# Expert rows added by token into a DRAM sum as they leave PSUM, router weights held stationary

## What is computed

```python
x = _layernorm(x + attention(x))
logits = x @ W_router.T                      # 2048 x 8
probs = softmax(logits)
rw, sel = top_k(probs, 2)
combine = zeros((T, 8)).at[arange(T)[:, None], sel].add(rw)
sh = silu_and_mul(x @ Ws_gate_up) @ Ws_down  # inner width 1408
shared_out = sh * sigmoid(x @ W_sgate.T)
h = silu_and_mul(einsum('th,ehi->eti', x, We_gate_up))   # inner width 352, eight experts
eo = einsum('eti,eih->eth', h, We_down)
x = _layernorm(x + shared_out + einsum('eth,te->th', eo, combine))
```

## Time and profile before

| | us |
|---|---|
| median of 3 runs (lowest, highest) | 1134.67 (1134.11, 1134.91) |
| profiled execution: its own time | 1130.08 |
| profiled execution: span, first to last instruction | 1128.2 |
| PE busy in the span | 1054.4 (93%) |
| DVE busy | 767.7 (68%) |
| ACT busy | 632.9 (56%) |
| POOL busy | 412.1 (37%) |

### The profile page before, as it was taken

How to read it: one execution, slowest core, us unless ns; L and a number is a source line. 1 busy time by engine, 2 the same in 40 slices (tenths; PEclk the granted TensorE clock), 3 DMA queues, 4 the chain that set the end, 5 groups by cost and what they waited for, 6 DMA issues and landing times.

```text
span 1128.2 us, 19960 instructions
## 1 busy us (share of the span) xinstructions
PE 1054.4 (93%) x7180; PEld 874.4 (78%) x7180; DVE 767.7 (68%) x1173; ACT 632.9 (56%) x1287; POOL 412.1 (37%) x546
## 2 busy tenths in 40 slices
PE   4899999999999859998999999999999999999964
PEld 3677777777777648887888888888888888888853
DVE  4888787787777742593767676776867677773434
ACT  4566666666666633233565666666666666653333
POOL 4577887787777620001000010010001001004783
PEclk8899999999999996899899999999999999999988
DMA  5111111111111014135777898887888888856993
GB/s 198 42 39 31 31 31 37 53 31 31 31 31 49 20 30 139 38 122 186 225 255 241 258 280 291 256 266 260 261 263 262 289 270 260 266 170 162 234 185 110
DMA packets 125760, 175.80 MB, mean 156 GB/s; under 512 B 10624, under 2 KB 64256, under 8 KB 125664
## 3 DMA queue, kind: packets, MB, share of 16 engines
q1 hardware_dynamic: 117936, 155.92, 44.2%
q0 software_dynamic: 7728, 18.62, 7.0%
HBM read 155.90 MB, written 18.61 MB: 155 GB/s over the span
## 4 chain that ended last, share of the span: by engine, by line
PE 57%; DVE 2%; issue 1%; DMA 1%; ACT 0%; SPq 0%; POOL 0%; POOLq 0%; DVEq 0%; ACTq 0%
PE gate_ps L1299 4%; PE gate_ps L1300 3%; PE gate_ps L1301 3%; PE up_ps L1300 3%; PE up_ps L1301 3%; PE up_ps L1299 3%; PE down_ps L1326 3%; PE down_ps L1325 3%; PE down_ps L1324 3%; PE e_up_ps L1350 3%; PE e_up_ps L1351 2%; PE e_up_ps L1352 2%; PE e_gate_ps L1359 2%; PE e_up_ps L1359 2%; PE e_up_ps L1361 2%; PE e_gate_ps L1361 2%
## 5 line engine op out<-in xcount | busy, mean ns | idle before, releaser
L886 POOL DMA_INDIRECT rows<-x_dram,token_i x39 | 40.4, 1036 | 519.8 <-PE e_gate_ps L1341 424.0
L1182 DVE TENSOR_TENSOR e_lo<-e_raw,e_hi 128x1408 fp32r<-128x1408 f32 x78 | 126.5, 1623 | 45.8 <-ACT e_hi L955 45.8
L955 ACT CAST e_hi<-e_raw 128x1408 fp32r<-128x1408 f32 x78 | 107.5, 1379 | 55.8 <-PE e_up_ps L1361 55.8
L316 ACT ACTIVATE prob<-score_ps,nbias 128x256 f32<-128x256 f32 x256 | 119.8, 478 | 8.7 <-DVE nbias L412 8.6
L256 POOL TENSOR_TENSOR probT<-probT,masks 128x256 f32<-128x256 f32 x128 | 97.4, 782 | 67.1 <-DVE probT L433 67.0
L1187 DVE TENSOR_TENSOR ed_lo<-ed_raw,ed_hi 128x1024 fp32r<-128x1024 f32 x39 | 47.8, 1225 | 70.4 <-ACT ed_hi L963 70.4
L412 DVE TENSOR_REDUCE nbias<-score_ps 128x2 f32<-128x512 f32 x128 | 88.4, 691 | 4.4
L1299 PE MATMUL gate_ps<-x_hi,gu_lo 128*128 128x512 f32 x176 | 73.7, 419 | 18.0 <-issue 11.8
L324 ACT COPY probT<-probT_ps 128x512 f32<-128x512 f32 x64 | 37.6, 587 | 92.9 <-PE probT_ps L540 92.9
L506 PE MATMUL proj_ps<-wqkv_lo,xT_hi 128*128 128x512 f32 x180 | 79.4, 441 | 0.0
L904 POOL DMA_INDIRECT x1T<-expert_rows,slot_i x32 | 52.5, 1639 | 55.8 <-DMA expert_rows<-rows 45.2
(11 more groups left out here) (221 smaller groups left out, 2982.9 us busy)
## 6 DMA issues: line engine op xcount, KB each, us to landing
e_raw<-in_We_gu SPq DMA_DIRECT2D x78, 704.0 KB, 4.6
ed_raw<-in_We_down SPq DMA_DIRECT2D x39, 512.0 KB, 4.1
raw_ring<-in_Ws_gu SPq DMA_DIRECT2D x58, 256.0 KB, 5.5
wd_raw<-in_Ws_down SPq DMA_DIRECT2D x44, 256.0 KB, 5.0
expert_rows<-rows SPq DMA_DIRECT2D x39, 256.0 KB, 2.1
gu_raw<-in_Ws_gu SPq DMA_DIRECT2D x30, 256.0 KB, 5.0
ed_raw<-in_We_down SPq DMA_DIRECT2D x39, 192.0 KB, 4.7
xT_in<-in_xT SPq DMA_DIRECT2D x16, 256.0 KB, 2.8
```

What stands on the lines that cost most here:

```text
L316: nc.scalar.activation(prob[:, g % 2, h, :], score_ps[:, h, 0:2 * P], ACT.Exp, bias=nbias[:, s % 2, head:head + 1], scale=1.0, accum_out=r ...
L955: nc.scalar.copy(e_hi[:, half * HK:(half + 1) * HK, :], raw_half(i, half)).then_inc(e_hi_made, 1)
L1182: nc.vector.tensor_tensor(e_lo[:, part, :], raw_half(i, half), e_hi[:, part, :].bitcast(FP32), ALU.subtract).then_inc(e_lo_made, 1)
```

## The change

**Adding by token.** The result rows of a tile are no longer stored by slot and gathered at the end. A new DRAM tensor `sum_dram` holds one row a token, and 128 more for unused slots. `begin_sums` copies x into it at down 2, and `add_rows(i)` on POOL adds each tile's rows to it by an indirect DMA that scatters, right after the row is made. Each add waits for the one before. The token numbers for it (`target_i`) are `token_i`, with unused slots sent to the extra rows. At the end `load_sums` loads the sums of a quarter (1 MB) into `e_raw` by one plain DMA, at down 36 to 39, and POOL adds them to the shared part (`take_sums`) for the first three quarters, DVE for the last (`add_last`). The shared part leaves `down_ps` by ACT instead of DVE. The norm's numbers are made for a whole quarter, with `STATS_AT` = 38.

**Router.** `router_parts` holds a 128x32 block of router weights (`r_wide`, nine columns and zeros) stationary and moves 512 tokens. The four k-blocks of a quarter go to four groups of 32 PSUM partitions, so that the sum over k is left open; `take_parts` copies the banks to SBUF, and `join_logits` makes the sum and the transpose in one step, with 16 matmuls of nine columns (`join`). The parts run ahead of gate 0, the join after it.

**Earlier index.** `PREFIX_AT` goes from 3 to 2 and `INDEX_AT` from 7 to 6; `FIRST_TILE_AT` stays 9.

```diff
-    PREFIX_AT, INDEX_AT, FIRST_TILE_AT, STATS_AT = 3, 7, 9, 37
-
-    slots_dram = nc.dram_tensor("expert_rows", (TILES * P, H), FP32, kind="Internal").ap()
+    PREFIX_AT, INDEX_AT, FIRST_TILE_AT, SUMS_AT, STATS_AT = 2, 6, 9, 36, 38
+
+    sum_dram = nc.dram_tensor("sum_dram", (S + P, H), FP32, kind="Internal").ap()
...
+            def begin_sums():
+                sp.dma_start(sum_dram[0:S, :], x1_dram).then_inc(sum_begun, 16)
+                sp.dma_start(sum_dram[S:S + P, :], x1_dram[0:P, :]).then_inc(sum_begun, 16)
+
+            def load_sums(tt):
+                sp.wait_ge(rows_added, 16 * TILES)
+                if tt >= 2:
+                    sp.wait_ge(sum_taken, BT * (tt - 1))
+                at = tt % 2 * BT
+                sp.dma_start(sums[:, at:at + BT, :], sum_dram[tt * TN:(tt + 1) * TN, :].rearrange("(b p) n -> p b n", p=P)).then_inc(sum_loaded[tt], 16)
...
-            def store_rows(i):
-                sp.wait_ge(row_made, i + 1)
-                sp.dma_start(slots_dram[i * P:(i + 1) * P, :], rows[:, 2 + i % 2, :]).then_inc(rows_stored[i % 2], 16)
...
+            sp.wait_ge(r_cleared, 1)
+            sp.dma_start(r_wide[:, :, 0:NR], W_router_gate.rearrange("(k p) n -> p k n", p=P)).then_inc(router_loaded, 16)
+            sp.dma_start(tables[:, :], ident_in).then_inc(tables_loaded, 16)
             load_raw(1)
...
-                if stage == "down" and n % UN == 3:
-                    load_y(n // UN)
+                if stage == "down" and n == 2:
+                    begin_sums()
...
+                if stage == "down" and SUMS_AT <= n < SUMS_AT + NT:
+                    load_sums(n - SUMS_AT)
+                if stage == "down" and STATS_AT + 2 <= n < STATS_AT + 2 + NT - 1:
+                    for b in range(BT * (n - STATS_AT - 2), BT * (n - STATS_AT - 1)):
                         store_out(b)
...
+            def add_rows(i):
+
+                pool.wait_ge(row_made, i + 1)
+                if i:
+                    pool.wait_ge(rows_added, 16 * i)
+                pool.indirect_dma_start(sum_dram, bass.IndirectOffsetOnAxis(ap=target_i[:, i:i + 1], axis=0), rows[:, 2 + i % 2, :], None,
+                                        compute_op=ALU.add).then_inc(rows_added, 16)
+
             for i in range(TILES):
                 if i >= 2:
                     pool.wait_ge(xeT_mm, i - 1)
                 pool.indirect_dma_start(rows[:, i % 2, :], None, x1_dram, bass.IndirectOffsetOnAxis(ap=token_i[:, i:i + 1], axis=0)).then_inc(xe_loaded[i % 2], 16)
...
+                if i >= 2:
+                    add_rows(i - 2)
+            for i in range(TILES - 2, TILES):
+                add_rows(i)
+
+            def take_sums(tt):
+
+                pool.wait_ge(sum_loaded[tt], 16)
+                pool.wait_ge(evacuated, BT * (tt + 1))
+                for b in range(BT * tt, BT * (tt + 1)):
+                    nc.gpsimd.tensor_tensor(y_block(b), y_block(b), sums[:, b % (2 * BT), :], ALU.add).then_inc(sum_taken, 1)
...
+            for tt in range(NT - 1):
+                take_sums(tt)
+            for tt in range(NT - 1):
+                rstd_of(quarter(tt))
+                for b in quarter(tt):
+                    shift_of(b)
+            for b in quarter(NT - 1):
+                rstd_of([b])
+                shift_of(b)
...
             def copy_row(i):
                 act.wait_ge(ed_mm, i + 1)
                 if i >= 2:
-                    act.wait_ge(rows_stored[i % 2], 16 * (i // 2))
+                    act.wait_ge(rows_added, 16 * (i - 1))
...
+            def evacuate(b):
+
+                act.wait_ge(down_mm, BT * (UN * (b // BT) + UN - 1) + b % BT + 1)
+                act.wait_ge(x_lo_made, KT * (b // BT + 1))
+                act.wait_ge(part_mm, NT)
+                nc.scalar.activation(y_block(b), down_ps[b % BT][:, :], ACT.Identity, scale=shared[:, b:b + 1]).then_inc(evacuated, 1)
...
+            def router_parts():
+
                 pe.wait_ge(router_loaded, 16)
+                for tt in range(NT):
+                    for k in range(KT):
+                        lanes = slice(k * (P // KT), (k + 1) * (P // KT))
+                        last = nc.tensor.matmul(down_ps[tt][lanes, :], r_wide[:, k, :], x1T[:, k, tt * TN:(tt + 1) * TN], start=True, stop=True)
+                    last.then_inc(part_mm, 1)
+
+            def join_logits():
+
+                pe.wait_ge(part_taken, NT)
+                pe.wait_ge(tables_loaded, 16)
                 for b in range(NB):
-                    for k in range(KT):
-                        last = nc.tensor.matmul(e_up_ps[:, b * NR:(b + 1) * NR], x1T[:, k, b * P:(b + 1) * P], r_raw[:, k, :], start=(k == 0), stop=(k == KT - 1))
+                    last = nc.tensor.matmul(e_up_ps[:, b * NR:(b + 1) * NR], logit_parts[:, b * P:(b + 1) * P], join, start=True, stop=True)
                 last.then_inc(logit_mm, 1)
```

More of the change, by code:

```diff
@@ new lines, in rstd_of, with shift_of @@
+            def rstd_of(blocks):
+                n, done = len(blocks), len(blocks) + blocks[0]
+                part = slice(blocks[0], done)
+                pool.wait_ge(y_mv, done)
+                nc.gpsimd.tensor_scalar(rstd[:, part, 1], mv[:, part, 1], 1.0, LN_EPS, ALU.mult, ALU.add).then_inc(y_var, n)
+                pool.wait_ge(y_var, done)
+                nc.gpsimd.tensor_tensor(rstd[:, part, 0], rstd[:, part, 1], half[:, 0:n], ALU.pow).then_inc(y_rstd, n)
+            def shift_of(b):
+                pool.wait_ge(y_rstd, b + 1)
+                nc.gpsimd.tensor_scalar(rstd[:, b, 2:3], mv[:, b, 0:1], rstd[:, b, 0:1], -1.0, ALU.mult, ALU.mult).then_inc(y_shift, 1)
@@ L1232, in _ @@
                     if n == 0:
-                        router_logits()
-                        router_probs()
-                    if n == 1:
                         router_top()
-                    for b in range(2 * (n - STATS_AT), 2 * (n - STATS_AT + 1)):
-                        if 0 <= b < NB - BT:
+                    tt = n - STATS_AT
+                    if 0 <= tt < NT - 1:
+                        for b in range(BT * tt, BT * (tt + 1)):
                             statistics(b)
-                if stage == "down" and n == 0:
-                    router_hits()
                 if stage == "down":
```

167 lines of the change are left out of this document (76 added, 91 removed).

## The result

The changed kernel takes 1097.49 us (median of 4 runs, 1094.26 to 1098.39) against 1134.39 (4 runs, 1134.03 to 1134.91): a ratio of 0.9675, 95% interval 0.9656 to 0.9695. It is 3.25% faster; 1098.2 was forecast.

What follows compares the result with a forecast made beforehand. PE, busy 93% of the span, was taken as the bound. Gains of 19.5 (router), 1.3 (first tile) and 15.7 (last units) sum to 36.5 us: 1130.1 to 1093.6 profiled, 1098.2 us as median; range 1091 to 1111.

Steps and rivals of the forecast that it cites:

- the clock fell at the join: Sign of being wrong: granted clock falls after the router's join; a fall was given a third, at 2 us.
- ACT waited 1.76 us at `normalise`: Sign of being wrong, in the last units: ACT waiting at `normalise`, where the forecast had nothing to wait for.
- Router: Start of the feed-forward part: wide parts and join replace 64 matmuls, gaining 19.5 us, bounds 7.6 and 22.7.
- First tile: PE's 5.6 us stall behind `e_lo`: the earlier index lets `xe_hi` start earlier, gaining 1.3 us, between 0 and 3.
- Last units: Units after gate 39: both PE waits and both slow starts go, gaining 15.7 us, with 3.4 us slack.
- DRAM copy: At down 2, 4.5 MB through SP's queue in 15 to 29 us: cost 0, unless above some 33 us.
- Tiles: Expert tiles: an adding scatter replaces the plain store, DMA share 0.83 to 0.88, time change 0.
- prediction's own threshold of 3 us: In the tiles: above 3 us of all DMA engines for each add, the tiles are bound by DMA.
- Groups in sequence: Rival, router parts: column groups do not overlap, parts take 19.3 instead of 6.7 us, total 1111; chance 0.12.
- Late sums: Rival, last units: slow loads of sums make gate 42 2 to 3 us late, total 1103; chance 0.13.
- Slower by DMA: Rival, tiles: adds into DRAM fill the DMA engines, 1157 at 4.5 us each; chance 0.08, of which slower 0.03.
- Index worth nothing: Rival, first tile: expert loads late anyway or index delays DVE, bringing nothing or costing 1 to 4 us, 1101; chance 0.07.

Runs made afterwards that it cites:

- early_router_load: Changed kernel with r_wide cleared at the start of attention and loaded behind the first gate and up weights: 1089.28 us, ratio 0.9621.
- late_index: Changed kernel with only the earlier index undone (PREFIX_AT 3, INDEX_AT 7): 1097.85 us, ratio 0.968.
- sums_alone: Changed kernel with the old router and old places of prefix and index, keeping the adds by token and plain loads of sums: 1115.84 us, ratio 0.9839.
- double_add: Changed kernel with each tile's rows also added, by a second indirect DMA, into another DRAM tensor nothing reads: 1091.8 us, ratio 0.9646.
- plain_scatter: Changed kernel with the scatter into the DRAM sum overwriting instead of adding: 1094.79 us, ratio 0.9667.
- join_twice: early_router_load with the 16 matmuls of the join made twice in a row: 1100.36 us, ratio 0.9702.
- more_code: Changed kernel with two one-column memsets added on POOL behind each tile's add, 78 in all: 1096.49 us, ratio 0.9672.

## Why the prediction was right

The time was 1097.49 for 1098.2, and each term of the sum held within 2 us. That the time came within 0.7 us is luck: the runs of the changed kernel lie 4.1 us apart, and the stretches gained 35.1 us for the 36.5 forecast. In two terms (router and tiles) the size was right and a part of the reasoning was not. Two of the prediction's own signs of being wrong came, both small: the clock fell at the join, and ACT waited 1.76 us at `normalise`.

- **Router, 19.5 us forecast.** 17.6 in the trace, 18.0 by undoing it. The start was right (parts 4.6 us behind the last transposes, forecast the same), the parts took 5.74 us for 6.7. A pass at full clock is 107 ns and not the 132 taken from the earlier trace rows, and the clock was low for about 4.4 us where 5 were counted; the 1.0 us won there pays for a part of what follows. **The step that was mis-sized is the clock at the join**: a third of 2 us was counted; it cost 0.8 us in the join and 2.4 in up 0. Without the fall, as in early_router_load, the step is as forecast (3.49 us for 3.5). By the rule of the Trainium skill (TensorEngine Tiling, "Instruction Overhead") the join would be 1 us; at full clock it is 0.109 us a pass, and the rule is wrong by 2.5 us here.
- **First tile, 1.3 us forecast.** 1.8 in the trace, of which 1.27 is waiting. The reason given is borne out by late_index: there ACT waits 5.2 us for that load of raw weights again, and PE 6.3 us for `e_lo`.
- **Last units, 15.7 us forecast.** 15.2, and 15.2 in sums_alone. The schedule counted from gate 37 (1023.54 now): third load of sums issued at 21.2 (forecast 21.2), its quarter taken at 32.3 (32.2), first shift at about 35 (33.2), `silu` ready at 38.7 (37.4), slack 2.1 us (3.4). The 1.3 us lie in the norm's numbers, 2.8 us where 1 was counted; ACT's four `normalise` and `silu` took 0.4 us less than counted. The third load landed in 5.6 us, as taken. The middle value in the earlier trace rows is not that of the four loads of line 795, which landed in 5.6, 7.9, 9.0 and 11.4 us; the argument, three of four above 7.5, stands. What of the gain is owed to the adds of rows being gone and what to the norm's numbers being made by the quarter, no run takes apart.
- **DRAM copy, 0.** Landed in 15.2 us (forecast 15); gate 1 to gate 8 is as before.
- **Tiles, 0.** Right in the time, wrong in the reasoning. The share is 0.93 for 0.88; the add took 2.5 us of the engines by the share, not 1.5. By the prediction's own threshold of 3 us that was near the bound; double_add reaches a share of 1.00 and loses no time, so the threshold was no bound.
- **The rivals.** Groups in sequence: did not come. The exchanged loops cost 1 to 3 us and not 13, but there two passes still ran together; 32 passes strictly one by one would take some 16 us, an estimate from 0.43 us a pass at full clock, twice that in the first 4.4 us, against the 19.3 forecast. Late sums: did not come, but the chain is as real as said, with 2.1 us of slack. Slower by DMA: did not come; its price per add was near the threshold and the threshold wrong. The page DMA: Bandwidth & Descriptors of the Trainium skill ("Rules for kernel authors") says that an accumulate reads its destination; plain_scatter's 15.3% against 26.5% agrees with it. Index worth nothing: against it stand the traces, with 2.3 us from attention to the end; the medians can't tell.

The medians gained 36.9 us, the stretches 35.1. The profiled execution of the kernel before was 4.3 us below its median, that of the changed one 0.4 above; what made the difference in the executions without a profile is not seen.

## What to carry to other kernels

Count a short wait or a thin stretch of PE with what stands behind it: in early_router_load 2.2 us of waiting less came with 6 us of gain, since the clock held through the next thin stretch, and in join_twice, with the same short wait, it did not hold. A count in a window is no rate where instructions overlap; take the starts. Where a stall is a chain of small steps on two engines, moving one of them moves the stall; look at what else stands ahead of the last step on each queue. And don't take a bound from adding up DMA shares: test it by doubling the transfer.

## What was not expected of the hardware

Some of DVE's subtractions were slower beside POOL's additions. Two timelines of the changed kernel, first DVE where POOL adds (from 1031.25 on), then where it does not:

```profile
1031.46 1.78 DVE L1203 TENSOR_TENSOR h_lo<-hidden,h_hi 128x512 fp32r<-128x512 f32 x1
```

```profile
1039.63 0.69 DVE L1203 TENSOR_TENSOR h_lo<-hidden,h_hi 128x512 fp32r<-128x512 f32 x1
```

The subtraction takes 1.78 us instead of 0.69, three more of its kind are slower beside POOL too (up to 2.08 us for 1.23), and POOL's four additions take 6.09 instead of about 5.5. Not all are: the split of wd at 1043.43 took 0.78 us beside POOL's additions, and `hidden`, with an input in PSUM, 0.69. The statistics of a block, with one input, stay at 0.66 to 0.69 us beside them. That POOL's additions are the cause is inferred from the times alone. It cost PE nothing here. And the end of attention, the same instructions in every kernel but for the clearing and loading of `r_wide` in three of them, moved by 4.9 us between profiles. The granted clock goes with it: 0.86 in the first 50 us and 0.71 from 400 to 417 us where it came at 422.00, 0.93 and 1.00 in more_code, where it came at 417.15.
